# One product of ones for the bias sums, and one transpose shared by the third tile's adapter columns and the opening tile's routing, in a fused AdaLN-FFN kernel

## What is computed

```python
y = x @ W.T + b1 + (x @ A[slot]) @ B[slot] * 2.0        # slot = itok[sequence], rank 16, 32 slots
base   = y @ base_w.T + b2
hidden = y @ A2.T                                        # rank 64
probs  = softmax(y @ router_w.T)                         # 16 experts
topw, topi = top_k(probs, 2); topw /= topw.sum() + 1e-6
combine = one_hot(topi) * topw, summed over the two
delta  = einsum("bse,bsr,eor->bso", combine, hidden, B2)
out    = x + base + delta * 0.5
```

## Time and profile before

| | |
|---|---|
| median of 3 runs | 101.2 us (101.11, 102.17, 101.2) |
| profiled execution, its own time | 101.23 us |
| its span | 99.4 us |
| granted TensorE clock | 1.0 of full speed in all slices |
| busy: PE, PEld, DVE, ACT, POOL | 95.7, 87.2, 66.1, 41.8, 22.2 us |
| DMA | 16.91 MB, mean 170 GB/s |

### The profile page before, as it was taken

One profiled execution on the slowest core, in us unless ns is written; L12 is line 12 of the kernel. 1 busy time (PEld: TensorE's weight loads), 2 busy tenths in 40 slices (PEclk: granted clock), 3 DMA queues, 4 the chain that ended last, 5 costly groups with the idle time before them and its releaser, 6 DMA issues.

```text
span 99.4 us, 1810 instructions
## 1 busy us (share of the span) xinstructions
PE 95.7 (96%) x572; PEld 87.2 (88%) x572; DVE 66.1 (67%) x183; ACT 41.8 (42%) x102; POOL 22.2 (22%) x34
## 2 busy tenths in 40 slices
PE   6899999999999999999999999999999999999990
PEld 6799999999999999998898799888787887878980
DVE  5669995997475885998977577257949275572101
ACT  3615526968787545756422610451424022040000
POOL 4100004325999965109122000000000000000000
PEclk9999999999999999999999999999999999999999
DMA  2999569899457786882590736416307465020211
GB/s 37 356 364 391 174 125 377 265 366 361 121 91 191 196 257 142 229 233 47 175 300 25 206 127 178 138 35 196 109 20 199 134 170 147 0 105 0 105 59 53
DMA packets 8379, 16.91 MB, mean 170 GB/s; under 512 B 1507, under 2 KB 4067, under 8 KB 8370
## 3 DMA queue, kind: packets, MB, share of 16 engines
q1 hardware_dynamic: 7762, 16.41, 54.5%
q10 hardware_dynamic: 576, 0.39, 1.2%
q0 software_dynamic: 32, 0.00, 0.0%
HBM read 13.28 MB, written 2.16 MB: 155 GB/s over the span
## 4 chain that ended last, share of the span: by engine, by line
PE 93%; DMA 3%; DVE 0%; ACT 0%; issue 0%
PE pair L819 90%; DMA w_raw_all<-w_cat 3%; PE pair L964 1%; PE pair L966 1%; PE pair L984 1%; DVE xn L813 0%; ACT w_hi_all L421 0%; PE pair L954 0%; PE pair L943 0%; PE pair L941 0%; PE pair L933 0%
## 5 line engine op out<-in xcount | busy, mean ns | idle before, releaser
L819 PE MATMUL pair<-e_hi,w_hi_all 128*128 128x512 f32 (+1 forms) x72 | 27.1, 376 | 0.0
L819 PE MATMUL pair<-e_hi,w_lo_all 128*128 128x512 f32 (+1 forms) x72 | 26.7, 370 | 0.0
L819 PE MATMUL pair<-e_lo,w_hi_all 128*128 128x512 f32 (+1 forms) x72 | 26.7, 370 | 0.0
L536 ACT ACTIVATE w_hi_all<-exp_raw_all 128x512 fp32r<-128x512 f32 x16 | 9.7, 630 | 15.3 <-DVE exp_raw_all L754 15.3
L819 PEld LDWEIGHTS pair<-e_hi,w_lo_all 128*128 128x128 f32 x72 | 13.5, 188 | 2.5
L819 PEld LDWEIGHTS pair<-e_hi,w_hi_all 128*128 128x128 f32 x72 | 13.6, 188 | 2.5
L819 PEld LDWEIGHTS pair<-e_lo,w_hi_all 128*128 128x128 f32 x72 | 13.6, 189 | 2.0
L761 DVE TENSOR_TENSOR w_lo_all<-exp_raw_all,w_hi_all 128x512 fp32r<-128x512 f32 x16 | 10.4, 688 | 4.5 <-ACT w_hi_all L536 3.9
L754 DVE TENSOR_TENSOR exp_raw_all<-w_raw_all 128x512 f32<-128x512 f32 x16 | 11.1, 735 | 0.2 <-DMA w_raw_all<-spill 0.2
L768 DVE TENSOR_TENSOR xn<-pair,xn 128x512 f32<-128x512 f32 x7 | 4.8, 690 | 9.1 <-PE pair L819 9.1
L819 PE MATMUL pair<-p_hi,x_hi 128*128 128x304 f32 x32 | 10.0, 311 | 0.0
(11 more groups left out here) (108 smaller groups left out, 162.5 us busy)
## 6 DMA issues: line engine op xcount, KB each, us to landing
w_raw_all<-spill SPq DMA_DIRECT2D x16, 256.0 KB, 4.0
xt_raw<-x_t SPq DMA_DIRECT2D x4, 512.0 KB, 6.0
exp_raw_all<-experts SPq DMA_DIRECT2D x4, 512.0 KB, 8.7
xn<-x_n SPq DMA_DIRECT2D x4, 512.0 KB, 5.0
out<-xn SPq DMA_DIRECT2D x7, 256.0 KB, 3.4
w_raw_all<-w_cat SPq DMA_DIRECT2D x2, 552.0 KB, 5.9
c_stack<-c_hi SPq DMA_DIRECT2D x7, 74.0 KB, 3.5
c_stack<-c_lo SPq DMA_DIRECT2D x7, 74.0 KB, 3.9
```

What stands on the lines that cost most here:

```text
L536: nc.scalar.activation(gt_hi[:, t % 2, js, :], g[:, js, :], ACT.Copy).then_inc(gh_done, 1)
L819: return nc.tensor.matmul(out_ap, lhs, rhs, start=first, stop=last)
```

## The change

The bias's partial sums are first folded from 128 to 64 partitions: ACT copies the upper 64 partitions of bias_part down (bias_up), DVE adds the lower 64 to them, ACT writes the high part into partitions 0 to 63 of bp_split, and DVE the low part into partitions 64 to 127. One product of ones over the 128 partitions sums both. routing_transpose(0) now takes all 128 columns, so tile 2's adapter columns with it; it is issued within x_other(2), ahead of chunk k = 2, and lora_transpose(2) is gone. ACT copies tile 2's adapter columns out of that transpose, in the same place of its program as before (after exps(1)). Further: on DVE bias_part_of(2) stands before folded_lo(0) where it stood after folded_lo(3); on ACT x_hi_part(2) stands ahead of the last folded_hi and waits for all four foldings; the low rows of c_first are copied from c_lo in SBUF, and x_first(1) no longer waits for them; lora_hi(4) waits for the shared transpose in place of its own.

```diff
         bias_part = sb("bias_part", [P, W2N])
-        bp_hi = sb("bp_hi", [P, W2N], F32R)
-        bp_lo = sb("bp_lo", [P, W2N], F32R)
+        bias_up = sb("bias_up", [P // 2, W2N])
+        bp_split = sb("bp_split", [P, W2N], F32R)
...
-            for n in range(KC):
+            for n in range(KC - 1):
                 folded_hi(n)
             act.wait_ge(in_xt[1], 16)
+            act.wait_ge(pe_p, KC)
             x_hi_part(2)
+            folded_hi(KC - 1)
             x_hi_part(3)
             split_experts(0)
+            act.wait_ge(bias_step, KC)
+            nc.scalar.activation(bias_up[:, :], bias_part[P // 2:, :], ACT.Copy).then_inc(bias_moved, 1)
             act.wait_ge(pe_c, 1)
             nc.scalar.activation(c_hi[:, :], w2_cols(ps_c), ACT.Copy).then_inc(ch_done, 1)
-            act.wait_ge(bias_step, KC)
-            nc.scalar.activation(bp_hi[:, :], bias_part[:, :], ACT.Copy).then_inc(bph_done, 1)
+            act.wait_ge(bias_added, 1)
+            nc.scalar.activation(bp_split[0:P // 2, :], bias_up[:, :], ACT.Copy).then_inc(bph_done, 1)
...
-                if t in (3, 4):
-                    act.wait_ge(pe_ht, t - 1)
-                elif t >= 5:
+                if t == 3:
+                    act.wait_ge(pe_ht, 2)
+                elif t >= 4:
                     act.wait_ge(pe_rt, t - 3)
...
             exps(1)
-            lora_t_alone(2)
+            lora_t(2, ps_rt[T_H:P, :])
...
             bias_part_of(1)
+            bias_part_of(2)
             folded_lo(0)
...
             folded_lo(3)
-            bias_part_of(2)
             bias_part_of(3)
+            dve.wait_ge(bias_moved, 1)
+            nc.vector.tensor_tensor(bias_up[:, :], bias_part[0:P // 2, :], bias_up[:, :],
+                                    ALU.add).then_inc(bias_added, 1)
             dve.wait_ge(ch_done, 1)
...
             dve.wait_ge(bph_done, 1)
-            nc.vector.tensor_tensor(bp_lo[:, :], bias_part[:, :], bp_hi[:, :].bitcast(F32),
+            nc.vector.tensor_tensor(bp_split[P // 2:, :], bias_up[:, :], bp_split[0:P // 2, :].bitcast(F32),
                                     ALU.subtract).then_inc(bpl_done, 1)
...
             lora_first_lo()
             dve.wait_ge(first_set, 2)
-            dve.wait_ge(first_high, 1)
-            nc.vector.tensor_tensor(c_first[F_LOW:F_LOW + R, :], w2_cols(ps_c)[0:R, :],
-                                    c_first[0:R, :].bitcast(F32), ALU.subtract).then_inc(first_low, 1)
+            dve.wait_ge(cl_done, 1)
+            nc.vector.tensor_copy(c_first[F_LOW:F_LOW + R, :], c_lo[0:R, :]).then_inc(first_low, 1)
...
                 elif t == 1:
                     pe.wait_ge(cl_done, 1)
-                    pe.wait_ge(first_low, 1)
...
-                x_side(t, out_cols, cols, bias_within=t == 0).then_inc(pe_x, 1)
+                x_side(t, out_cols, cols, within=t in (0, 2)).then_inc(pe_x, 1)
...
-                    if k == KC - 1 and bias_within:
+                    if k == KC - 1 and t == 0 and within:
                         bias()
+                    if k == 2 and t == 2 and within:
+                        routing_transpose(0)
...
-                halves(ps_b, BANK - W2H, W2H, ones[:, :], bp_hi[:, :], True, False)
-                halves(ps_b, BANK - W2H, W2H, ones[:, :], bp_lo[:, :], False, True).then_inc(pe_bias, 1)
+                halves(ps_b, BANK - W2H, W2H, ones[:, :], bp_split[:, :], True, True).then_inc(pe_bias, 1)
...
-                if t >= 2:
-                    pe.wait_ge(ht_again_done, t - 1)
-                    pe.wait_ge(rt_done, t - 1)
...
-                if 3 <= t + 2 < NT:
+                if t + 2 < NT:
                     cols = P
...
             x_first(2)
-            routing_transpose(0)
             lora_product(1)
             x_other(2)
-            lora_transpose(2)
             x_first(3)
```

More of the change, by code:

```diff
@@ L209, in adaln_ffn_kernel @@
         bias_step = sem("bias_step")
+        bias_moved = sem("bias_moved")
+        bias_added = sem("bias_added")
         bph_done = sem("bph_done")
@@ L904, in x_other, with x_side @@
                 out_cols, cols = other_half[t % 2]
-                x_side(t, out_cols, cols, bias_within=t == 0).then_inc(pe_x, 1)
-            def x_side(t, out_cols, cols, bias_within=False):
+                x_side(t, out_cols, cols, within=t in (0, 2)).then_inc(pe_x, 1)
+            def x_side(t, out_cols, cols, within=False):
                 par = t % 2
```

## The result

The changed kernel takes 101.91 us (median of 22 runs, 101.37 to 102.54) against 101.38 of the kernel before (22 runs, 100.87 to 102.63). The ratio is 1.0046, with a 95% interval of 1.0025 to 1.0066: slower, by a little less than half a per cent, where 0.2 us less was forecast. (The prediction called anything within about 1% the same; that part of it held.) The profiled execution took 101.59 us, with a span of 99.5.

The account below looks back on a forecast made before the run. PE bounds the kernel, busy 95.7 of 99.4 us, so each removed matmul counts whole: 101.23 - 0.27 (bias pass) - 0.11 (transpose) + 0.19 (wait at x_first(4)) = 101.04 us, range 100.8 to 101.6.

Parts of the forecast that it names:

- PE's own work: On PE through tile 2: one bias pass (0.27) and one transpose (0.11) go, 0.38 us less.
- The bias chain: Folding up to PE's bias weight load: sums 1.3 us earlier, low part 0.08 ahead of the load; wait 0, bounds 0 and 0.2.
- the chain behind the shared transpose: From transpose through exps(1) and MAX8 (0.46 later) to tile 2's acc_done (35.95, was 35.81): PE waits 0.19, bounds 0.05 to 0.5.
- x_first(4) waits for just that: At x_first(4)'s weight load: tile 2's acc_done, at 35.95, is all it waits for; a wait of 0.19 us.
- rival C: Near x_first(4): POOL's x_lo_part(4) goes ahead of split_experts_lo(2) and holds it 1.09, giving 102.13 us; chance 0.08.
- I take 0: Behind the bias: copying c_first's low rows from SBUF fits DVE's idle time and costs PE 0.
- worst case: Behind the bias: POOL's x_lo_part(3) starts first, holds the copy 1.09; stack_bias 0.30 later, opening product waits 0.24.
- A: Rival at x_first(4): no new wait of PE at all, 100.85 us; chance 0.15.
- B: Rival at the bias: chain late by 0.2, 101.24 us; held copy of c_first's low rows, up to 0.24, included; chance 0.17.
- D: Rival in the experts' stage: gain is there, but the first weigh waits on the late spread, 101.2 to 101.9 us; chance 0.05.

Follow-up runs that it names:

- e11: Changed kernel with split_experts_lo(2) behind route(2), the product of ones one matmul later, GpSimd's lora_a_parts(2) ahead of x_lo_part(3); stretch 75.50 us, ratio 0.9993.
- e1: Changed kernel with VectorE's split_experts_lo(2) moved from ahead of lora_lo(3) to behind route(2); stretch 75.61 us, ratio 1.0013.
- e3: Changed kernel with both transposes as in the kernel before, so only the bias part of the change; stretch 76.20 us, ratio 1.0044.
- e4: Kernel before with only the shared transpose of the change, the bias as it was; stretch 76.08 us, ratio 1.0023.
- e2: Kernel before with VectorE's split_experts_lo(2) moved behind route(2); stretch 75.92 us, ratio 0.9986.
- e10: Kernel before with two semaphores more, which nothing uses; stretch 75.92 us, ratio 1.0027.
- e5: As e3, but c_first's low rows by the old subtraction out of PSUM, x_first(1) waiting for it again; stretch 75.92 us, ratio 1.0025.

## Why the prediction was wrong

What it forecast of PE's own work held: 0.38 was to go, and e11, without waits, is 0.41 shorter. The bias chain was right to a tenth: counted from x_first(0)'s start the sums were complete 1.26 earlier (19.61 + 0.83 = 20.44, forecast 1.3), the late steps took as long on 64 partitions as on 128 (0.77 for the addition), and the weight load came 0.10 later (23.62 - 20.72 against 23.76 - 20.96), inside the bounds of 0 and 0.2 where 0 was taken. So was the chain behind the shared transpose. Counted from x_first(0)'s start, MAX8 came 0.62 later than before (forecast 0.46) and acc_done 0.24 later (forecast 0.14); alone it would have made x_first(4) wait 0.17, where 0.19 was forecast.

The step that failed is "x_first(4) waits for just that". x_first(4) also waits for the eighth count of x_done, which GpSimd's x_lo_part(4) raises, and in the kernel before that came at 35.84, 0.03 behind acc_done. The prediction followed VectorE's split to acc_done, and had read in the earlier trace rows that VectorE and GpSimd hold each other off, even that x_lo_part(4) comes due in just that place. It asked only whether GpSimd could delay VectorE (rival C), and not what VectorE's later split does to GpSimd. x_lo_part(4) ended 0.60 later than before (15.48 against 14.88 from x_first(0)), PE wanted it 0.26 earlier in that count, and the 0.36 that it had before its use (35.84 to 36.20) became an idle time of 0.55 of the weight load.

The second step is "I take 0" for the copy. Its own worst case came true in kind: GpSimd started x_lo_part(3) at 23.59, when VectorE still had lora_first_lo to do, and the copy of 23.75 took 1.44 (less than the 1.09 + 0.78 of the worst case, since it is 0.46 by itself). The forecast looked for the price at stack_bias and the opening product. That was 0.06 (L954 took 0.36 in place of 0.30). The larger price was on GpSimd, whose next cast was held by the copy in turn: 0.24 on the chain that sets x_first(4).

The sum with its terms as measured: -0.41 (as in e11) + 0.10 (bias) + 0.06 (opening product) + 0.55 (x_first(4)) = 0.30, which is the stretch's difference. The forecast had -0.38, 0, 0 and 0.19, or -0.19 in all: it missed the stretch by 0.49. The bounds were drawn for the waits that were followed, and the kernel before had a second, equally tight one.

That the range ended at 101.6 and excluded 101.91 has two more reasons. With 0.49 more the forecast of 101.04 would be 101.53, still inside, though the upper part of the range was meant for sums of other waits. About 0.2 lies outside the span, which had no row before the change; its cause stays open, so some two fifths of the timed loss are not explained. And the kernel before itself took 101.38 in the median of 22 runs, 0.15 above the execution from which the forecast started.

The rivals: A (no wait) did not come. B's two parts were both real, 0.10 and 0.06, and both small; what the held copy cost by way of GpSimd was in no rival. C did not happen: with GpSimd first it would have shown as a split of over 2 us, and in the changed kernel it took 1.22. D did not happen; PE has no wait in the experts' stage, in the changed kernel or in e1.

## What to carry to other kernels

Where an engine is full and a few instructions are taken out of it, list for each of its following waits every semaphore with its time, and not only the one that came last: two that lie 0.03 apart are one wait, with two chains behind it. Where two engines can hold each other off, price a shift in both directions, and follow the small instruction that is held to whatever stands behind it in its queue. And with gains of tenths in executions that differ by one microsecond, compare a stretch that begins behind the noise: here it repeats within 0.01.

## What the runs showed of the hardware that was not expected

- VectorE's copy of 16 x 592 from SBUF to SBUF takes 0.46 alone and 1.44 when GpSimd's 128x512 subtraction has begun; GpSimd's 128x64 cast takes 0.24 alone and 0.48 behind that copy, and GpSimd's 128x512 subtraction 1.29 alone and 2.32 when VectorE's 128x1024 one began 0.05 before it. Behind one and the same VectorE split of 128x1024 a cast of 128x64 took 1.24 in place of 0.24 (e3), a subtraction of 128x64 1.34 in place of 0.32 (changed kernel) and one of 128x512 2.32 in place of 1.29 (e4): 1.0 more each time, whatever the size of the held instruction. The Trainium skill, SBUF — State Buffer, section "Who interferes with whom", says that issue order and not the form of the operation decides who is blocked; the runs agree, for subtractions, casts and this copy: in each pair the operation that took longer than by itself is the one that started later.
- The same fold products of PE step at 0.14 per matmul in some executions almost from the start, and in others at 0.25 up to 6.8 us. In e2 this made the product that starts at 7.84 in the kernel before start at 8.78, 0.94 later. The profile's granted clock reads 1.00 in all windows of both. It is not the only thing that differs between executions: in e10 the first products step at 0.14, and a wait of 0.95 for ScalarE (L435) at 8.74 makes x_first(0) as late as in e2.
- The time outside the span was 1.74 to 1.85 us in all 116 executions of the kernel before that were timed with the experiments, and in all 24 of e2 and e10. In the changed kernel it is near 1.8 in some and near 2.1 in others (22 executions, mean 1.98), and so in every variant with another PE program (the highest is 2.49, in e5), in e4 too, which has no semaphore or instruction more. All of these have another ScalarE program as well, so which engine's program it goes with is not told apart; e2, where only VectorE's differs, has 1.8. The two semaphores are not the cause. What the cause is stays open.

e10 is the kernel before with them:

```diff
         bias_step = sem("bias_step")
+        sem("bias_moved")
+        sem("bias_added")
```

> The kernel before with two semaphores more, which nothing uses. In the changed kernel and in all variants with another PE program the execution's time lies 1.8 us above the span in some executions and 2.1 in others; in the kernel before it is 1.8 in all. If the two semaphores make this, the time outside the span has both values here too and the ratio is 1.001 to 1.002. If not, it is 1.8 in all executions and the ratio is 1.000. The stretch is 75.91 either way.

In e10 it was 1.76 to 1.84 in all twelve, with a stretch of 75.92.
